# Cross-attention block on one core: sampled maxima of a slot in one stretch with half the keys, another order of the first fetches, a later check of the sums

## The reference

```
x = layer_norm(hidden, ln1_w, ln1_b)                      # 8 x 256 x 256
q = x @ q_w + q_b;  k = ctx @ k_w + k_b;  v = ctx @ v_w + v_b   # ctx 8 x 1601 x 256, 16 heads of 16
scores = where(mask, q k^T / 4, min)
out = softmax(scores) v
hidden = out @ cproj_w + cproj_b + hidden
y = layer_norm(hidden, ln2_w, ln2_b)
return hidden + gelu(y @ fc_w + fc_b) @ proj_w + proj_b    # inner width 1024
```

## Time and profile before

| | us |
|---|---|
| median of 3 runs | 695.26 (694.9 to 695.87) |
| profiled execution, time | 695.34 |
| its span | 693.6 |
| PE busy | 654.5 |
| ACT busy | 441.2 |
| DVE busy | 365.8 |
| POOL busy | 124.9 |

### The profile page before, as it was taken

The page is one execution under the profiler, slowest core; times in us unless marked ns, Lnnn a source line. Parts: engine busy times, 40 slices in busy tenths (PEclk is TensorE's granted clock), DMA queues, the critical chain, the costliest instruction groups (busy, mean ns, idle before and its releaser), DMA issues.

```text
span 693.6 us, 16715 instructions
## 1 busy us (share of the span) xinstructions
PE 654.5 (94%) x7026; PEld 465.5 (67%) x7026; DVE 365.8 (53%) x786; ACT 441.2 (64%) x469; POOL 124.9 (18%) x102
## 2 busy tenths in 40 slices
PE   3757999999999999999999999999999999998997
PEld 3644666666666676667667666666666555797897
DVE  4854655754455445544554455445744331766763
ACT  7305667777777777677767776777677899512320
POOL 6421031203120312031203120312000431011000
PEclk9988999999999999999999999999999999999999
DMA  8967484448454845483548364736443700000001
GB/s 280 286 231 253 162 271 160 169 160 284 148 183 181 257 141 196 161 272 131 209 172 266 116 231 162 256 112 235 153 168 112 311 3 2 0 31 16 17 31 35
DMA packets 51354, 113.76 MB, mean 164 GB/s; under 512 B 6923, under 2 KB 40067, under 8 KB 49995
## 3 DMA queue, kind: packets, MB, share of 16 engines
q1 hardware_dynamic: 40660, 81.07, 34.7%
q10 hardware_dynamic: 10614, 31.57, 12.7%
HBM read 65.30 MB, written 47.06 MB: 162 GB/s over the span
## 4 chain that ended last, share of the span: by engine, by line
PE 85%; ACT 5%; DMA 4%; DVE 2%; SPq 1%; ACTq 1%; issue 1%; POOL 0%; POOLq 0%
PE O L1248 27%; PE U L1163 22%; PE S L1241 17%; PE S L1163 5%; ACT pr L656 4%; PE U L1356 3%; PE O L1356 3%; DMA k_scr<-kpart 3%; PE S L1229 2%; PE U L1292 2%; PE U L1218 2%; DVE g_lo L998 1%; DMA q_scr<-qpart 1%; DMA cols_s<-in_cols 1%; PE U L1209 1%
## 5 line engine op out<-in xcount | busy, mean ns | idle before, releaser
L656 ACT ACTIVATE pr<-S 128x1024 f32<-128x1024 f32 x416 | 396.2, 1028 | 171.5 <-PE S L1241 171.5
L1248 PE MATMUL O<-pr,vsl 128*17 128x256 f32 x3328 | 211.1, 382 | 0.0
L1241 PEld LDWEIGHTS S<-qst,kst 64*128 64x128 f32 x1664 | 110.0, 186 | 78.1 <-issue 44.1
L1241 PE MATMUL S<-qst,kst 64*128 64x256 f32 x1664 | 147.0, 301 | 6.8 <-ACT pr L656 3.3
L1248 PEld LDWEIGHTS O<-pr,vsl 128*17 128x17 f32 x3328 | 81.5, 97 | 83.7 <-issue 17.0
L870 DVE TENSOR_REDUCE mx<-S 128x4 fp32r<-128x1024 f32 x64 | 77.6, 1216 | 41.7 <-PE S L1229 41.6
L573 POOL CAST c_hi<-cT 128x768 fp32r<-128x768 f32 (+1 forms) x28 | 24.7, 883 | 316.6 <-DMA cT<-in_ctx_t 166.0
L813 DVE TENSOR_SCALAR kpart<-U,cols_s 128x384 fp32r<-128x384 f32 (+1 forms) x60 | 37.5, 626 | 76.5 <-PE U L1163 76.2
L822 DVE TENSOR_TENSOR vsl<-U,rows_s 128x256 f32<-128x256 f32 (+1 forms) x91 | 34.6, 418 | 79.3 <-PE U L1163 79.2
L578 POOL TENSOR_TENSOR c_lo<-cT,c_hi 128x768 fp32r<-128x768 f32 (+1 forms) x32 | 60.9, 1905 | 6.5 <-ACT c_hi L651 4.3
L1163 PE MATMUL U<-c_hi,w_hi 128*128 128x384 f32 (+1 forms) x120 | 47.9, 399 | 13.8 <-POOL c_lo L578 11.8
(11 more groups left out here) (126 smaller groups left out, 795.8 us busy)
## 6 DMA issues: line engine op xcount, KB each, us to landing
kst<-k_scr SPq DMA_DIRECT2D x87, 400.2 KB
k_scr<-kpart SPq DMA_DIRECT2D x48, 384.0 KB, 3.6
v_scr<-vsl ACTq DMA_DIRECT2D x8, 1768.0 KB, 6.0
cT<-in_ctx_t ACTq DMA_DIRECT2D x21, 384.0 KB, 4.3
k_scr<-kpart SPq DMA_DIRECT2D x16, 449.0 KB, 2.6
qst<-q_scr SPq DMA_DIRECT2D x90, 64.0 KB
q_scr<-qpart SPq DMA_DIRECT2D x16, 256.0 KB, 2.5
cT<-in_ctx_t ACTq DMA_DIRECT2D x7, 449.0 KB, 4.6
```

The lines of the kernel that those rows point to most:

```text
L656: nc.scalar.activation(pr[:, DEEP * ((GROUPS * b + g) % 2) + i, :], S[:, 2 * i:2 * i + 2, :] .rearrange("p a n -> p (a n)"), ACT.Exp).then ...
L1241: last = nc.tensor.matmul(S[:, 2 * i + g_, j * LQ:(j + 1) * LQ], kst[rows_, s, j, kt * P:(kt + 1) * P], qst[rows_, s, j, :], start=True, s ...
L1248: last = nc.tensor.matmul(O[32 * h:32 * h + VW, 0:LQ], vsl[:, par, s, kt, h * VW:(h + 1) * VW], pr[:, buf, h * LQ:(h + 1) * LQ], start=kt ...
```

## The change

It has four parts.

1. `max_unit` and `max_evac` take a whole slot: eight matmuls with 128 keys each, one reduction over the same 128 x 1024 elements, then the transpose. `max_of` gives them in the fourth group of a slot only (MAX_AT = 3), and for slot 1 of the first batch row in group 1 of that row.
2. In the head, slot 1's and slot 2's fetches go to SP's queue, slot 1's right behind slot 0's. The four stores of half 1 and two of the loads of context go to ACT's queue, behind a wait for slot 0 to have landed.
3. The mask's row is made on ACT, before the constant rows, with a bias that DVE works out (8 x 1).
4. The check of the sums: the small reduction stays in the second token group, the product and the rest go to the third; PE waits for DVE's reduction before the transposes of the fourth.

```diff
-SAMPLE = 256
+SAMPLE = 128
-HEAD_MAX = [(s, j) for s in range(2) for j in range(NJ)]
+HEAD_MAX = [0]
+MAX_AT = 3
 def max_of(b, g):
+    if (b, g) == (0, 1):
+        return 0, 1
     s, k = divmod(g, SLOTG)
     b_, s_ = b + (s + 2) // SLOTS, (s + 2) % SLOTS
-    return (b_, s_, k // 2) if len(steps_of(g)) < DEEP and b_ < B else None
+    return (b_, s_) if k == MAX_AT and b_ < B else None
...
             fill_mask(sp, first, 0, 0)
-            for c in range(CH):
-                store_k(0, 1, c)
+            first_fill(sp, 0, 1)
             first_rows(0, 0)
+            first_fill(sp, 0, 2)
             first_rows(0, 1)
...
-            next_ctx(1, 2)
-            zero(5)
-            next_ctx(1, 3)
-            zero(6)
-            zero(7)
+            for i in range(4, SLOTS * NJ):
+                zero(i)
+            act.wait_ge(mask_steps, 4)
+            nc.scalar.activation(mk_f, mk_f, ACT.Identity, bias=some_b[:, 2:3], scale=MASKED).then_inc(mask_steps, 1)
             act.wait_ge(kst_zeroed, SLOTS * NJ)
             constant_rows(act)
-            first_fill(act, 0, 1)
-            first_fill(act, 0, 2)
+            act.wait_ge(first.slot_in[0], 16 * FILLS)
+            for c in range(CH):
+                store_k(act, 0, 1, c)
+            next_ctx(1, 2)
+            next_ctx(1, 3)
...
-            def max_evac(b, s, j, use, i):
+            def max_evac(b, s, use, i):
                 dve.wait_ge(peak_ready, use + 1)
-                nc.vector.tensor_reduce(mx[:, s % 2, :, j:HG:NJ].rearrange("p q g -> p g q"),
-                                        S[:, 2 * i:2 * i + 2, :].rearrange("p g (q k) -> p g q k", q=QT), AX.X, ALU.max,
-                                        negate=True).then_inc(peak_taken, 1)
+                nc.vector.tensor_reduce(mx[:, s % 2, :, 0:HG].rearrange("p q h -> p h q"),
+                                        S[:, 2 * i:2 * i + 2, :].rearrange("p g (j q k) -> p (g j) q k", j=NJ, q=QT),
+                                        AX.X, ALU.max, negate=True).then_inc(peak_taken, 1)
...
+                        if s_ is first and c == 1 and i == 4:
+                            check_rows()
-                        if s_ is first and c == 1 and i == 4:
+                        if s_ is first and c == 2 and i == 3:
                             checked()
...
-            def max_unit(b, s, j, i):
-                for q in range(QT):
-                    for g_ in range(2):
+            def max_unit(b, s, i):
+                for j in range(NJ):
+                    for q in range(QT):
+                        for g_ in range(2):
+                            rows_, at = slice(g_ * HALF, g_ * HALF + MAXROW), (j * QT + q) * SAMPLE
...
-                if i < 2:
-                    pe.wait_ge(peak_taken, len(HEAD_MAX) - 1 + i)
+                if i == 0:
+                    pe.wait_ge(peak_taken, 1)
+                elif i == 1:
+                    pe.wait_ge(xb_taken, 9)
...
                         if i == 5 and c + 1 < NTG:
+                            if s_ is first and c == 2:
+                                pe.wait_ge(good_steps, SLOTS * B + 3)
                             turn_y(s_, c + 1)
-                        if s_ is first and c == 1 and i == 7:
-                            pe.wait_ge(first.yt_done, KC * (c + 2))
+                        if s_ is first and c == 2 and i == 1:
+                            pe.wait_ge(first.yt_done, KC * (c + 1))
```

More of the change, by code:

```diff
@@ L480, in _ @@
             sp.dma_start(some[:], some_scr[0].partition_broadcast(P)).then_inc(some_in, 16)
-            store_k(0, 0, 0)
-            store_k(0, 0, 1)
-            store_k(0, 0, 2)
+            store_k(sp, 0, 0, 0)
+            store_k(sp, 0, 0, 1)
+            store_k(sp, 0, 0, 2)
             sp.wait_ge(kst_zeroed, SLOTS * NJ)
@@ L487, in _ @@
             store_q(0)
[L488 to L489 removed]
+            store_k(sp, 0, 0, 3)
+            sp.wait_ge(mask_steps, 5)
             sp.dma_start(mask_scr, mk_f).then_inc(mask_out, 16)
@@ L863, in q_evac @@
                                         ).then_inc(ql_done, 1)
-            def max_evac(b, s, j, use, i):
+            def max_evac(b, s, use, i):
                 dve.wait_ge(mx_zeroed, 1)
-                if j == 0 and SLOTS * b + s >= 2:
+                if SLOTS * b + s >= 2:
                     dve.wait_ge(mrow_done, SLOTS * b + s - 1)
                 dve.wait_ge(peak_ready, use + 1)
-                nc.vector.tensor_reduce(mx[:, s % 2, :, j:HG:NJ].rearrange("p q g -> p g q"),
-                                        S[:, 2 * i:2 * i + 2, :].rearrange("p g (q k) -> p g q k", q=QT), AX.X, ALU.max,
-                                        negate=True).then_inc(peak_taken, 1)
-                if j == NJ - 1:
-                    if b > 0 or s >= 2:
-                        dve.wait_ge(first.mrow_in[(s + 2) % SLOTS], ROWS_IN * (b if s < 2 else b + 1))
-                    dve.wait_ge(peak_taken, use + 1)
-                    turn_rows(s).then_inc(mrow_done, 1)
+                nc.vector.tensor_reduce(mx[:, s % 2, :, 0:HG].rearrange("p q h -> p h q"),
+                                        S[:, 2 * i:2 * i + 2, :].rearrange("p g (j q k) -> p (g j) q k", j=NJ, q=QT),
+                                        AX.X, ALU.max, negate=True).then_inc(peak_taken, 1)
+                if SLOTS * b + s >= 2:
+                    dve.wait_ge(first.mrow_in[(s + 2) % SLOTS], ROWS_IN * (b if s < 2 else b + 1))
+                dve.wait_ge(peak_taken, use + 1)
+                turn_rows(s).then_inc(mrow_done, 1)
             def turn_rows(s):
@@ L1220, in q_unit @@
                 last.then_inc(ready, 1)
-            def max_unit(b, s, j, i):
-                if j == 0:
-                    pe.wait_ge(first.slot_in[s], 16 * FILLS * (b + 1))
-                for q in range(QT):
-                    for g_ in range(2):
-                        rows_ = slice(g_ * HALF, g_ * HALF + MAXROW)
-                        last = nc.tensor.matmul(S[:, 2 * i + g_, q * SAMPLE:(q + 1) * SAMPLE], query_set(rows_, s, j, q),
-                                                kst[rows_, s, j, q * SAMPLE:(q + 1) * SAMPLE], start=True, stop=True)
+            def max_unit(b, s, i):
+                pe.wait_ge(first.slot_in[s], 16 * FILLS * (b + 1))
+                for j in range(NJ):
+                    for q in range(QT):
+                        for g_ in range(2):
+                            rows_, at = slice(g_ * HALF, g_ * HALF + MAXROW), (j * QT + q) * SAMPLE
+                            last = nc.tensor.matmul(S[:, 2 * i + g_, at:at + SAMPLE], query_set(rows_, s, j, q),
+                                                    kst[rows_, s, j, q * SAMPLE:(q + 1) * SAMPLE], start=True, stop=True)
                 last.then_inc(peak_ready, 1)
```

51 lines of the change are left out of this document (19 added, 32 removed).

## The result

The changed kernel takes 689.36 us (median of 4 runs, 689.21 to 689.49), the kernel before 695.57 us on the same chip (4 runs, 694.90 to 696.18): a ratio of 0.9908, with an interval of 0.9895 to 0.9922. A later repeat gave 689.31 against 695.62, 0.9913 (0.9895 to 0.9932). So the kernel became faster by 6.2 us, where 13.3 was forecast; 689.36 lies above the range. The profiled execution has a span of 687.7 us against 693.6.

The account below looks back on a forecast made before the run. TensorE was taken to bound the steady part, ScalarE the last batch row, and waits for slot 0 and its followers the head. Savings of 8.8 + 2.5 + 0.6 + 1.4 = 13.3 from 695.3 gave 682.0 us, range 677.5 to 688.5.

Parts of the forecast that it names:

- the head: Start of the kernel, up to group 3's maxima: forecast to bring -8.8 us, bounds -5.9 to -9.6.
- (a) to (c): Head: mask row's arithmetic on ACT, context loads later, nothing beside slot 0; slot 0 lands at 41.3, not 46.
- (d): Head: one reduction instead of two, rows ready at 43.8; with slot 1's bytes ahead of them, first scores at 48.0.
- (f): Head: exponentials, maxima, projection and values behind the first scores; group 3's maxima at 58.8 against 67.59.
- R1: Rival, 16%: in the head, stores beside slot 1 hold back slot 2 and rows; head -5, 685.8, or 688 with lower clock.
- Steady part: Maxima units between head and last batch row: one longer unit replaces two, -0.09 a slot over 28 slots, -2.5 us.
- The total of 689.4: Alternative total if 81 ns per matmul held in each half of the array: steady part +4.9 instead of -2.5.
- Last batch row: ACT's idle of 0.64 behind group 6's maxima goes with that unit: -0.6 us (0 to -1.2).
- Token groups: Check of the sums moved: -2.4 in the second group, loss of 1.0 in the third, net -1.4 us.

Follow-up runs that it names:

- e3: Changed kernel with ACT's four key stores and two context loads waiting for slot 0's maxima rows instead of for slot 0; 690.03 us.
- e4: Changed kernel with slot 0's maxima rows sent from ACT's queue, ahead of its key stores, instead of by SP; 688.03 us.
- e7: Changed kernel with the four key stores on SP, behind slot 0's rows and ahead of slot 2, and the context loads behind ACT's fifth exponential; 688.27 us.
- e8: e7 with DVE's second reduction of the check moved from behind unit 3 to behind unit 1 of the third token group; 688.94 us.
- e9: e8 with every slot's maxima placed behind group 1 of the slot before, SP's rows and stores following that order; 687.24 us.
- e13: e8 with slot 2's maxima alone moved from group 3 to group 6 of the first batch row; 684.38 us.
- e14: e13 with 18 filler products of constant weights on PE ahead of the first maxima; 684.49 us.
- e1: Changed kernel with the check of the sums put back to where it stood before, in the second token group; 689.74 us.
- e2: Changed kernel with SP issuing slot 0's maxima rows ahead of slot 1's fetch; 688.67 us.
- e6: Changed kernel with 56 filler products in PE's idle stretch ahead of the first scores; 689.97 us.
- e10: Changed kernel with only the two context loads moved, from behind ACT's key stores to behind the fifth exponential; 689.40 us.
- e11: Changed kernel with the eight products of a maxima unit done twice in the 30 units behind the head; 704.34 us.
- e12: The changed kernel run again, unaltered; 689.31 us.

## Why the prediction was right and wrong

Right were the direction, the places and most of the small terms; wrong was the head, and with it the size.

*Head, (a) to (c): right, the closeness by chance.* Mask row issued at 37.98 (37.8 forecast), slot 0 at 41.26 (41.3), rows ready near 44.0 (43.8). But thirteen executions of this head had slot 0 at 41.26 to 43.84, 42.3 in the middle, so the forecast was typically 1 us short.

*Head, (d): the step that failed.* "With slot 1's bytes ahead of them I take 48.0 for these": the first scores came at 52.26. The step put the rows' delay down to slot 1, which e3 shows to be harmless (6.1 us behind the landing with slot 1 ahead in the queue; the forecast implied 6.7), and left out the four key stores that the same change starts at 41.15 in ACT's queue. With the stores behind the rows it is 6.0 to 6.1 us in all seven kernels (e3, e4, e7, e8, e9, e13, e14); with the stores where the change has them it is 9.1 to 11.0 in all seven (the changed one, e1, e2, e6, e10, e11, e12). The packet records of the trace say where the time goes: the 16 packets of 256 bytes that make up the four rows pass from 47.97 to 51.64 us, while ACT's queue passes some 250 packets per microsecond. Each row's first packet passes 3.9 to 4.7 us after its issue; in e3, e4 and e7, without the stores, it is 1.1 to 1.3 us. How the engines choose between the queues is not shown. Cost: 4.3 us in this execution, 3.6 in e12 (first scores at 51.58).

*Head, (f): short by 1.2.* From the first scores to group 3's maxima 12.05 us instead of 10.8 (in e12 13.23, short by 2.4). The sum took maxima, projection and values at full clock; the granted clock was 0.50 from 52.3 to 59.6, behind a stretch of 5.56 us in which PE stood. That the clock costs is shown by e7 against e8 (2.7 us to group 2's scores); how much of the 1.2 here is due to it was not separated, since the fillers moved or shortened a stretch and removed neither. Together 5.5: the head brought 3.3 and not 8.8.

R1 named this mechanism ("hold back slot 2 and the rows") at 16%, at 685.8, or 688 with the lower clock. It is what happened, with a larger loss than it was priced at: the head brought 3.3 and not 5. The forecast itself took the same stores at nothing for the rows. Its other half, slot 2, was hidden in the changed kernel, as the rows were late by more; it came to light when they were cured (e7, e8), and e13 shows what it held: 684.38 without it.

*Steady part: right, a little less.* 68.71 to 68.455 us a batch row is 0.06 a slot and not 0.09, over 28 slots 1.8 and not 2.5. A further pair costs 0.117 (0.11 forecast). The four pairs of a unit start 0.064, 0.118 and 0.115 us apart, where the forecast had 0.11 three times, and from the last one to the next kind of product it is 0.21, where the forecast put a stream of 0.06. That 0.21 is not new: the units before had it too (0.334 from the first pair to the next kind), and the scores have it where no unit follows them, against 0.116 where one does. So a unit removed gives 0.334 + 0.116 - 0.21 = 0.24 (forecast 0.237), and the longer one costs 0.51 - 0.334 = 0.18 more: 0.06 a slot is left. The Trainium skill's page "TensorE: Matmul & The Clock Gate", section "Back-to-back issue gap", gives 81 ns for a matmul of 128 columns in a sustained stream, so 0.65 for the eight of a unit (an estimate from that page). The trace does not agree for products that run two at a time in the two halves of the array: e11's eight more cost 0.47, 58 ns each. The total of 689.4 that the prediction worked out by that rule is near the measured one by chance: the steady part moved by -1.8 and not by +4.9.

*Last batch row: -0.3, not -0.6.* The gap of 0.64 went, and the next one grew from 0.63 to 0.81.

*Token groups: right.* -2.3 in the second (-2.4 forecast), +1.2 in the third (+1.0), net -1.15 by e1's trace; e8 shows that 0.6 of the 1.2 was to be had back.

*End.* PE's last product starts 6.49 us sooner (682.24 against 688.73), the span ends 5.9 sooner; the 0.6 between is in the landing of the last outputs, in one execution each, and was not studied.

Sum: 3.3 + 1.8 + 0.3 + 1.15 - 0.6 = 5.95, against 5.9 in the spans and 6.2 in the medians.

Open: why slot 0's landing scatters, what the lower clock behind the first scores costs in the whole, and how it could be avoided; neither filler did it dependably.

## What to carry to other kernels

Before a small transfer that something waits for is priced, list every large transfer that will be in flight beside it on any queue, those that the change itself starts above all; the order within its own queue mattered nothing here, 1.6 MB in the other queue mattered 3 to 5 us. When several waits end close to each other, a cure for the first shows the next, so a gain should be priced only up to the next wait: here late rows, then ACT's issuing, then slot 2, and only e13 kept the gain. Move the need where the transfer can't be moved: putting one unit of work three groups later brought some 4 us (e8 to e13), where none of the orders of the queues in e2 to e4, e7 and e8 brought the changed kernel 2 us.

## What the runs showed of the hardware

- Four transfers of 1 KB, alone beside the tail of a 1.4 MB fetch, released their user 3.4 us after the first was issued (e3: 46.60 to 49.95). With 1.6 MB of stores in the other queue it was 8.2 us in the changed kernel (44.02 to 52.26), 6.4 in its repeat (e12: 45.16 to 51.58) and 6.3 with nothing ahead of them in their own queue (e2: 45.21 to 51.54). A row's first packet passed 1.1 to 1.3 us after its issue without the stores (e3, e4, e7) and 3.9 to 4.7 with them (changed kernel), while some 250 packets per microsecond of the other queue passed.
- The same program met two different clocks in the same stretch in two executions (e7 and e8, 52 to 55 us: 0.50 and 1.00), worth 2.7 us in that place.
- Filler did not remove a stretch at 1.2 GHz: 3.75 us of it in e6 put its start from 51.2 (e12) to 55.1 and left 6.8 us of 10.3; 2.32 us in e14 left 3.4 us of the 6.8 of the stretch it stood before, and the next one where e13 had it (49.9 and 50.0).
- Two row-tiled products of 128 columns, one in each half of the array, cost 0.117 us together, where two of 256 columns cost 0.12: half the columns bought next to nothing. The loads' 0.11 would explain it, and the first interval of a unit, 0.064, fits, if that pair's load was made behind the scores before it; that was not tested apart.
